# A ring of four weight slots and one spare, with gate and up loads sent ahead of down's

## What is computed

```python
E, H, I, TOPK = (16, 512, 352, 4)
perm = jnp.argsort(flat_expert)                       # rows sorted by expert
tok = jnp.repeat(jnp.arange(n_tokens), topk)[perm]
xs = x[tok]
gate = ragged_dot(xs, gate_weight.T, group_sizes)     # 512 -> 352, weights of the row's expert
up = ragged_dot(xs, up_weight.T, group_sizes)
down = ragged_dot(silu(gate) * up, down_weight.T, group_sizes)     # 352 -> 512
out = zeros.at[tok].add(down * w_sorted[:, None])
```

## Time and profile before

| what | us |
|---|---|
| median of 3 runs | 2156.8 (2156.68 to 2157.38) |
| profiled execution | 2163.69 |
| its span | 2161.5 |
| TensorE busy in the span | 1973.5 (91%) |
| GpSimd busy in the span | 567.5 (26%) |
| first gate and up product of this stage starts | 1887.54 |
| last gate and up product (tile 23) starts | 2125.35 |

### The profile page before, as it was taken

The page is one execution under the profiler, slowest core; times in us unless marked ns, Lnnn a source line. Parts: engine busy times, 40 slices in busy tenths (PEclk is TensorE's granted clock), DMA queues, the critical chain, the costliest instruction groups (busy, mean ns, idle before and its releaser), DMA issues.

```text
span 2161.5 us, 38438 instructions
## 1 busy us (share of the span) xinstructions
PE 1973.5 (91%) x14580; PEld 1560.8 (72%) x14580; DVE 1061.3 (49%) x2477; ACT 889.4 (41%) x1819; POOL 567.5 (26%) x416
## 2 busy tenths in 40 slices
PE   6989999996997999986899999999999999798886
PEld 6977777885446878774587777999989999633333
DVE  5546666764114366688747777333234555410111
ACT  4346666532223455566655544422253232211110
POOL 3333332322342211000031110333241110145553
PEclk9999999998998999997999999999999999899998
DMA  3200010238355221141020000222220000468895
GB/s 125 77 25 29 14 42 5 70 126 310 71 88 126 76 83 55 66 157 44 5 72 34 29 15 3 89 62 58 68 77 24 29 28 2 169 193 258 264 279 154
DMA packets 67918, 189.22 MB, mean 88 GB/s; under 512 B 15114, under 2 KB 16366, under 8 KB 62510
## 3 DMA queue, kind: packets, MB, share of 16 engines
q1 hardware_dynamic: 50606, 163.90, 22.5%
q0 software_dynamic: 17152, 23.10, 5.6%
HBM read 224.56 MB, written 20.91 MB: 114 GB/s over the span
## 4 chain that ended last, share of the span: by engine, by line
PE 75%; DVE 8%; DMA 7%; ACT 4%; issue 3%; SPq 1%; POOL 1%; ACTq 0%; DVEq 0%; POOLq 0%
PE psum L106 16%; PE psum L109 15%; PE psum L107 15%; DMA l3f_weights<-in_l3f_gate_up_dram 4%; PE psum L1580 4%; PE psum L900 3%; PE psum L3610 3%; PE psum L3578 2%; PE psum L2801 2%; PE psum L3596 2%; PE psum L1607 2%; PE psum L926 2%; PE psum L2447 1%; PE psum L3032 1%; PE psum L139 1%
## 5 line engine op out<-in xcount | busy, mean ns | idle before, releaser
L1580 PE MATMUL psum<-l3f_weights,l3f_x_turned 128*64 (+1 forms) x768 | 131.0, 498 | 30.6 <-issue 16.6
L1580 PEld LDWEIGHTS psum<-l3f_weights,l3f_x_turned 128*64 128x64 f32 x768 | 58.1, 148 | 94.2 <-issue 72.3
L2238 ACT ACTIVATE l2x_probs<-psum,l2x_shift 100x361 f32<-100x361 f32 x128 | 70.2, 562 | 97.3 <-DVE l2x_shift L2293 97.3
L1875 POOL TENSOR_TENSOR l2x_ctx_lo<-l2x_ctx_raw,l2x_ctx_hi 128x1448 fp32r<-128x1448 f32 x8 | 26.4, 3297 | 314.9 <-ACT l2x_ctx_hi L1883 314.9
L1676 DVE TENSOR_TENSOR l3f_h<-l3f_silu,psum 128x352 f32<-128x352 f32 x24 | 12.5, 522 | 164.4 <-ACT l3f_silu L1662 156.0
L3749 ACT ACTIVATE l0x_probs<-l0x_probs,l0x_lowest 100x361 f32<-100x361 f32 x128 | 75.2, 588 | 42.1 <-DVE l0x_lowest L3918 42.1
L106 PE MATMUL psum<-xn_hi,l2f_w_gu_hi 128*128 128x400 f32 x256 | 88.6, 346 | 1.6 <-DVE xn_lo L192 1.3
L448 POOL TENSOR_TENSOR l2f_w_gu_lo<-l2f_raw_gu,l2f_w_gu_hi 128x512 fp32r<-128x512 f32 x32 | 43.0, 1357 | 174.2 <-ACT l2f_w_gu_hi L463 174.2
L107 PE MATMUL psum<-xn_lo,l2f_w_gu_hi 128*128 128x400 f32 x256 | 87.8, 343 | 0.0
L2476 ACT ACTIVATE ln_squares<-l1x_clipped,l1x_key_shift,l1x_key_scale 128x400 f32<-128x400 f32 (+1 forms) x96 | 62.3, 712 | 51.4 <-DVE l1x_clipped L2515 51.4
L3918 DVE CUSTOM_DVE_ANT_0 l0x_probs<-psum,l0x_outside 100x361 f32<-100x361 f32 x128 | 62.9, 531 | 32.1 <-PE psum L3578 29.6
(11 more groups left out here) (553 smaller groups left out, 6120.9 us busy)
## 6 DMA issues: line engine op xcount, KB each, us to landing
l3f_weights<-in_l3f_gate_up_dram SPq DMA_DIRECT2D x24, 1408.0 KB
l3f_weights<-in_l3f_down_dram SPq DMA_DIRECT2D x24, 768.0 KB
l0x_w_raw<-in_slabs_dram SPq DMA_DIRECT2D x52, 256.0 KB, 2.6
l0f_weights<-in_slabs_dram SPq DMA_DIRECT2D x8, 1536.0 KB
l1x_piece<-in_bit_w_dram SPq DMA_DIRECT2D x8, 1024.0 KB, 6.4
l1f_raw<-in_bit_w_dram SPq DMA_DIRECT2D x8, 1024.0 KB, 8.3
l2f_raw_gu<-in_slabs_dram SPq DMA_DIRECT2D x32, 256.0 KB, 2.6
l0x_ctx_raw<-in_ctx_dram SPq DMA_DIRECT2D x8, 724.0 KB, 4.2
```

The costliest lines, as they stand in the source:

```text
L1580: mm = pe.matmul(c.psum[lanes, bank + x, 0:self.INNER], self.x_turned[:, t % 2, k, lanes], weights, start=k == 0, stop=k == KD - 1)
L1875: pool.tensor_tensor(self.ctx_lo[:, q, :, :], self.ctx_raw[:, :, :], self.ctx_hi[:, q, :, :], ALU.subtract).then_inc(self.s("ctx_split"), 1)
L2238: act.activation(self.probs[:, m % 2, g, :], c.psum[0:S, g, 0:C], ACT.Exp, bias=self.shift[:, g:g + 1], scale=self.SCALE, accum_out=self.t ...
```

## The change

The ring has four slots and there is one spare slot: the five slots stay the same memory. `load_ring` is split into the reading of the row number (`ring_row`), `load_gate_up` and `load_down`. `prefetch` still loads three tiles in full. `sync` now sends gate and up of tile 3 first and then, for each tile, gate and up of t+1 ahead of down of t. The constants follow `RING` and `SPARE`: the waits of `load_spare`, the table of places, and the semaphores by slot. GpSimd's and TensorE's orders are not touched.

```diff
-    RING, SPARE, ROWS = 3, 2, 3
+    RING, SPARE, ROWS = 4, 1, 3
...
-    def load_ring(self, c, sp, t):
+    def ring_row(self, sp, t):
+        return sp.value_load(self.ring_rows[0:1, t:t + 1], min_val=0, max_val=P * (self.experts - 1))
+
+    def load_gate_up(self, c, sp, t, at):
 
         q = t % self.RING
-        at = sp.value_load(self.ring_rows[0:1, t:t + 1], min_val=0, max_val=P * (self.experts - 1))
         wait(sp, self.s("gate_up_units"), t - self.RING + 2 if t >= self.RING else 0)
         sp.dma_start(self.weights[:, q, 0:self.DOWN_AT],
                      c.a["l3f_gate_up"][bass.DynSlice(at, P), :]).then_inc(self.s(f"gate_up_landed{q}"), 16)
+
+    def load_down(self, c, sp, t, at):
+
+        q = t % self.RING
         wait(sp, self.s("d_units"), t - self.RING + 2 if t >= self.RING else 0)
...
-        for t in range(self.RING):
-            self.load_ring(c, sp, t)
+        for t in range(self.RING - 1):
+            at = self.ring_row(sp, t)
+            self.load_gate_up(c, sp, t, at)
+            self.load_down(c, sp, t, at)
...
-        for t in range(self.RING, self.TILES):
-            self.load_ring(c, sp, t)
+        at = self.ring_row(sp, self.RING - 1)
+        self.load_gate_up(c, sp, self.RING - 1, at)
+        for t in range(self.RING - 1, self.TILES):
+            this, at = at, None
+            if t + 1 < self.TILES:
+                at = self.ring_row(sp, t + 1)
+                self.load_gate_up(c, sp, t + 1, at)
+            self.load_down(c, sp, t, this)
```

## The result

| | before | changed |
|---|---|---|
| median, us (4 runs each) | 2156.7 (2155.6 to 2157.4) | 2293.9 (2291.5 to 2295.1) |
| ratio, 95% interval | | 1.062 (1.060 to 1.065) |
| profiled execution / span | 2163.7 / 2161.5 | 2294.6 / 2292.2 |
| gate and up products, TensorE busy / idle before them | 131.0 / 30.6 | 173.2 / 117.2 |

By the medians the change costs 137 us, 6.4%; the ratio and its interval say 6.0 to 6.5%. The two spans differ by 130.7 us, and the groups of TensorE's instructions hold all of it: 86.6 us more idle time before the gate and up products, 42.2 us more time in them, and 2.0 us before the last down product. Groups by line of the changed kernel: busy us, mean ns of one, idle before, releasers.

What follows compares the result with a forecast made beforehand. TensorE and DMA were both read as near full in the last stage. A new period of 8.31 + 4.8 + 2.1 = 15.2 us against 10.59 added 105.3 us in all: 2269.0 profiled, 2262 by the median, range 2208 to 2312.

Steps and rivals of the forecast that it cites:

- the forecast case: Last stage: spare loads stall TensorE each tile and lower its clock; period 15.2 us, 2262 us by the median, chance 0.62.
- D: The end of a tile's down product on TensorE, from which the prediction counted the steps of the stall.
- The wake and the issues: After the down product: POOL wakes in 0.75 us, then two spare issues with their gap take 2.37; ends at D+3.12.
- The last step to TensorE: From the spare load's landing to the start of the next gate and up product: 0.1 us.
- The queue's term: Spare load's landing beside ring traffic: 0.8 us added for both queues wanting the same engines, making the stall D+4.8.
- The clock's term: Gate and up product after each idle wait: a lowered TensorE clock adds 2.1 us per tile, ends 0 and 2.9.
- The step to the median: From profiled execution to median of the runs: 6.9 us taken off, 2269.0 to 2262.
- Alone, this part would be worth about 30 us: Ring of four with gate and up ahead of down, alone: tile period falls from 10.59 to 9.1 us over 21 tiles.
- The DMA's floor of 9.1 us a tile: Last stage: ring, gathered rows and sums, 2.23 plus 0.52 MB per tile at 301 GB/s, need 9.1 us.
- the ring's rival: New TensorE spare wait vanishes, so the DMA's 9.1 us per tile bounds the last stage: 2128 us, chance 0.06.
- The short stall: Rival: spare loads land as on an idle queue and the clock holds; period 12.3 us, 2200 us, chance 0.17.
- The long stall: Rival: spare packets stand behind whole ring loads, some D+7.0; 17.6 us per tile, 2315 us, chance 0.15.

Runs made afterwards that it cites:

- the reordered kernel: Changed kernel with GpSimd issuing spare down of tile t behind spare gate and up of t+1: 2226.7 us, 1.031 against the kernel before.
- the kernel with TensorE kept busy: Changed kernel with 16 unused 128 x 128 identity products after turning h in every tile: 2259.5 us, 1.045 against the kernel before.
- the last kernel above: Kernel before with new load order, three spare slots, spare loads and gathers a tile further ahead, spare down before sums, four row buffers: 2122.2 us, 0.982.

## Why the prediction was right, and where it was not

The forecast was 2262 us with a range of 2208 to 2312; 2293.9 lies in it, but outside the forecast case's own 27 us.

- **The mechanism.** Shown: the spare chain of one slot ends the wait (leaving it out gives 0.982; the single slot alone gives 1.100), POOL's two issues stand directly behind D, and no product follows the ring's landing. GpSimd's order is half of it, as the reordered kernel shows.
- **The wake and the issues**, D+3.12, came as D+3.18 in the turn shown, which makes some 1 us in all.
- **The last step to TensorE, "0.1 for TensorE", was mis-sized.** From the end of the issue to the product 0.9 us were counted and 1.43 measured, so the unloaded stall is 4.6, not 4.0. The packets' end was taken for the landing, and no row stands behind the 0.1; without ring traffic it is 0.7. This is 0.5 to 0.6 us a tile, 12 us in all.
- **The queue's term** was 0.8 and is 1.0: another 5 us or so. That the spare packets find the end of a burst was right; that a few of them, perhaps one engine's, come half a microsecond or more behind the rest was not thought of. The first of them moved at least 1.6 us after the end of the first spare issue (2007.85 to 2009.5), near the 2 us named as a sign of a wrong size. The estimate by the Trainium skill's rule ("DMA: Bandwidth & Descriptors", "Queues, rings and completion order"), one packet's wait and D+4.1, fell short by 1.5 us; 0.5 of that is the landing.
- **The clock's term** was 2.1 and is 2.31, near the mean of the three waits over 2.9 us; with tile 1's product, which also ran slow (6.65), 6 us. That it is the clock is shown by the kernel with TensorE kept busy for 42 of the 52 us. "All three idle times over 2.9 us cost" is true of the rows but is no limit: in the same trace idle times of 2.67 (product at 1990.29) and 2.00 us (2082.05) gave 6.6 us products, while 3.46 us in the kernel with the new order alone (1937.72) left 4.95.
- **The last down product**: 2.86 us idle against the 0.94 before; 1.4 was forecast and 2.0 came, for the same landing. With this, the terms above are the 25 us by which the spans' difference was missed.
- **The step to the median.** I took 6.9 us off because the profiled execution before was that much above the median. After, it is 0.7 above. That offset belonged to one execution; 6 us of the 32 missing are this.
- **"Alone, this part would be worth about 30 us" failed.** The new order alone, and the ring of four with two spare slots, are 17 and 14 us slower than before by the ratio. The step read the late load in the earlier trace rows as the whole of the wait and gave the 1.6 us behind it to nothing. They were spare semaphores. With these left out on both sides the order gains about 20 us (2143.3 to 2123.6); the whole gain over the kernel before, 36 to 39 us against the runs beside them, is both together. "The new order holds nothing up and costs nothing" failed with it: what it holds up is not on SyncE but on GpSimd's queue, through the shared engines.
- **The DMA's floor of 9.1 us a tile was too high.** It rested on 301 GB/s at full use. From 1940 to 2060 us the last kernel above moves 314 to 322 GB/s in windows of 40 us with 0.99 to 1.00 of the engines' time busy, so 2.75 MB take about 8.6 us, and the 8.67 us of TensorE hold. The forecast's case did not use this floor, the ring's rival did.
- **A reading.** The least busy time of TensorE in the earlier trace rows is 17.05 us, not 17.4; nothing hangs on it.
- **The other rivals.** The short stall's landing was refuted by the kernel without ring loads, which has 4.6; its steady clock by the products' 7.26. The ring did not win. The long stall's price, D+7, was too low even for its own case, 10 us in the kernel with one slot and a ring of three.

Left open: why the last 18 spare packets come about half a microsecond or more behind the others, and whether they are one engine's. It was seen in single turns and not tried by itself.

## What to carry to other kernels

A transfer that moved nothing here still cost its issue, its packets and its semaphore, and the engine that waited for it waited for the chain in front of the issue: count for each issue in an engine's order which wait stands before it. When a wait ends with "issue" some tenths of a microsecond to 2 us behind the transfer named, look at the other semaphores of that wait; leaving one of them out shows which it was. Sending large loads earlier delayed the small transfers that share the DMA engines, so give these their lead first: here one tile more for spare loads and gathered rows turned the same order of loads from 0.8% slower into 1.8% faster.

## What the runs showed of the hardware

- An indirect load whose rows are all out of bounds takes 1.03 us of GpSimd and 144 packets, and releases its waiter 1.43 us after the end of its issue on a quiet queue (2.46 us from its start); beside the ring's loads it took 9.1 us from its start in the turn shown with two spare slots and a ring of four (2001.44 to 2010.54).
- TensorE, in the kernel without later ring loads, after 4.17 us idle in each turn ran its 4.95 us product in 6.3 to 8.0 us, in a pattern that repeats (6.65, 7.9, 6.65, 6.3, 7.7) though each idle time was the same: what the product lost depends on more than the idle time before it.
- With 0.92 of the DMA engines' time busy over 200 us the stage of the last kernel moved 290 GB/s, and 314 to 322 GB/s in its three windows from 1940 to 2060, and TensorE had no gap there.
